# Selecting condition weights in bf16 parts, and a new order for the start of an attention kernel

## The reference, cut to what matters

```python
# x: (32, 32, 512) = batch, channel, time; itok: (32,) in 0..15; all float32
W1 = L0_cond_weights[itok]                   # (32, 32, 32), chosen by the token of each batch
h = einsum('bct,bcd->bdt', x, W1)            # first mix
q, k, v = h @ wq, h @ wk, h @ wv             # 32 query heads, 8 key/value heads of 128
...                                          # rotary embedding, causal softmax, out = att @ v
x = x + out @ wo
W2 = L0_cond2_weights[itok]
y = einsum('bct,bcd->bdt', x, W2)            # second mix
x = x + ffn(y)                               # fp8 rounding of y and of the weight, bias, scale
```

## Time and profile before

| | |
|---|---|
| median of 3 runs | 549.89 us (548.65 to 551.2) |
| the profiled execution | 549.17 us |
| its span | 547.3 us, mean granted clock 0.976 |
| TensorE busy | 521.5 us, 95% of the span |
| VectorE busy | 354.2 us, 65% |
| GpSimd busy | 221.7 us, 40% |
| ScalarE busy | 211.1 us, 39% |
| DMA engines | q1: 26.63 MB, 14.0% of the time of 16 engines |

### The profile page before, as it was taken

One profiled execution on the slowest core, in us unless ns is written; L12 is line 12 of the kernel. 1 busy time (PEld: TensorE's weight loads), 2 busy tenths in 40 slices (PEclk: granted clock), 3 DMA queues, 4 the chain that ended last, 5 costly groups with the idle time before them and its releaser, 6 DMA issues.

```text
span 547.3 us, 8771 instructions
## 1 busy us (share of the span) xinstructions
PE 521.5 (95%) x3208; PEld 416.5 (76%) x3209; DVE 354.2 (65%) x544; ACT 211.1 (39%) x369; POOL 221.7 (40%) x178
## 2 busy tenths in 40 slices
PE   8799999999999999999999999999999999999690
PEld 6687888888888888888888888888888888887320
DVE  5658356666676667666666675667566756675697
ACT  1244224341634163416342535162516251612524
POOL 0035623542663266326722673267326633510002
PEclk9999999999999999999999999999999999999775
DMA  8404400020103010301020102010202000000004
GB/s 265 164 1 153 174 0 2 1 96 2 46 33 96 0 71 6 96 0 77 0 96 0 77 1 94 0 77 18 78 0 77 6 0 1 2 0 1 2 0 153
DMA packets 17662, 26.88 MB, mean 49 GB/s; under 512 B 1611, under 2 KB 5835, under 8 KB 17644
## 3 DMA queue, kind: packets, MB, share of 16 engines
q1 hardware_dynamic: 17644, 26.63, 14.0%
HBM read 24.53 MB, written 2.10 MB: 49 GB/s over the span
## 4 chain that ended last, share of the span: by engine, by line
PE 94%; DVE 4%; DMA 1%; issue 1%; ACT 0%; DVEq 0%; SPq 0%
PE bank L524 25%; PE bank L525 24%; PE bank L526 24%; PE bank L603 3%; PE bank L590 3%; PE bank L544 3%; PE bank L545 3%; PE bank L546 3%; PE bank L718 2%; PE bank L658 1%; PE bank L496 1%; PE bank L507 1%; DVE xacc L999 1%; PE bank L715 1%; DMA cst<-in_constants 1%; DVE v_all L994 1%
## 5 line engine op out<-in xcount | busy, mean ns | idle before, releaser
L814 DVE TENSOR_TENSOR q_cos<-bank,cst 128x512 f32<-128x512 f32 x80 | 55.3, 691 | 105.2 <-ACT q_swap L385 105.2
L293 POOL TENSOR_TENSOR q_rot<-q_cos,q_swap 128x512 f32<-128x512 f32 x64 | 82.5, 1289 | 89.2 <-DVE q_swap L816 89.2
L524 PE MATMUL bank<-wo_hi,o_hi 128*128 128x512 f32 x256 | 101.6, 397 | 1.3 <-issue 1.3
L524 PE MATMUL bank<-hT_hi,wq_hi 128*128 128x512 f32 x256 | 101.3, 396 | 0.0
L525 PE MATMUL bank<-wo_lo,o_hi 128*128 128x512 f32 x256 | 99.8, 390 | 0.0
L525 PE MATMUL bank<-hT_lo,wq_hi 128*128 128x512 f32 x256 | 99.8, 390 | 0.0
L526 PE MATMUL bank<-wo_hi,o_lo 128*128 128x512 f32 x256 | 99.6, 389 | 0.0
L526 PE MATMUL bank<-hT_hi,wq_lo 128*128 128x512 f32 x256 | 99.6, 389 | 0.0
L384 ACT ACTIVATE q_swap<-bank 64x512 f32<-64x512 f32 x80 | 47.6, 595 | 127.3 <-PE bank L526 127.3
L859 DVE TENSOR_TENSOR xacc<-xacc,bank 128x512 f32<-128x512 f32 x64 | 43.4, 677 | 42.7 <-PE bank L526 42.5
L272 POOL TENSOR_TENSOR wo_lo<-raw_o,wo_hi 128x512 fp32r<-128x512 f32 x32 | 43.6, 1387 | 58.7 <-ACT wo_hi L374 58.7
(11 more groups left out here) (126 smaller groups left out, 716.1 us busy)
## 6 DMA issues: line engine op xcount, KB each, us to landing
raw_q<-in_L_attn_wq SPq DMA_DIRECT2D x8, 1024.0 KB, 5.8
raw_o<-in_L_attn_wo SPq DMA_DIRECT2D x8, 1024.0 KB, 5.0
xacc<-in_x SPq DMA_DIRECT2D x4, 512.0 KB, 7.3
raw_k<-in_L_attn_wk SPq DMA_DIRECT2D x8, 256.0 KB, 2.6
out<-xacc SPq DMA_DIRECT2D x8, 256.0 KB, 2.0
raw_o<-in_L_attn_wv SPq DMA_DIRECT2D x1, 1024.0 KB, 8.0
raw_q<-in_L_attn_wv SPq DMA_DIRECT2D x1, 1024.0 KB, 5.9
q_rot<-in_L_ffn_qweight SPq DMA_DIRECT2D x1, 1024.0 KB
```

The lines of the kernel that those rows point to most:

```text
L293: pool.tensor_tensor(dst, q_cos[b][:], q_swap[b][:], ALU.add).then_inc(rope_done, 1)
L524: pe.matmul(dst, l_hi, r_hi, start=(i == 0), stop=False)
L814: dve.tensor_tensor(by_t(q_cos[b][:]), by_t(q_ps[ITEM_BANK[k]][:]), cos_b, ALU.mult).then_inc(rope_cos, 1)
```

## The change

- The condition weights are split into three bf16 parts that add up to them exactly. ScalarE rounds (three casts), VectorE subtracts what has been rounded from `wcond` in place (two *remainder* steps). The parts lie side by side in `wcond_parts`, in `s_exp`.
- The selectors are bf16, which holds 0 and 1 exactly. select(i) is eight bf16 matmuls of 192 columns (3 parts of 64). In spread_first VectorE first adds the three parts with a reduction into `chosen` (in `p_tr`) and then spreads from there; the late spreads read `chosen` too, and no longer PSUM. The fourth select uses bank 3 again and not bank 7.
- ScalarE issues the loads of the small constants and of the condition weights; SP starts with the tokens and goes on with `x`. The first half of the value weights comes in two loads of 512 KB, each behind one of the first two pairs of `x`, with a semaphore of its own.
- The low parts of the first half of the value weights are made by GpSimd, and ScalarE makes the high parts in pairs between the first h_high.
- The orders: TensorE has select 0, mix 0, 1, select 1, mix 2, 3, select 2, values 0, 1, select 3, mix 4, 5, values 2. values(0) no longer waits for the late spreads. VectorE's order is below.

The core of the diff:

```diff
-        sel_ps = [bank[3], bank[4], bank[5], bank[7]]
+        sel_ps = [bank[3], bank[4], bank[5], bank[3]]
...
-            sp.dma_start(cst[:, 0:C_FIRST], consts[:, 0:C_FIRST]).then_inc(dma_cond, 16)
-            sp.dma_start(wcond, cond_v).then_inc(dma_cond_w, 16)
             for t in range(0, TILES, 2):
                 sp.dma_start(xacc[:, t:t + 2, :], x_rows[t:t + 2].rearrange("t p h -> p t h")).then_inc(dma_x[t // 2], 16)
-                if t == 2:
-                    sp.dma_start(raw_o[:], wv_v[:, :, 0:512]).then_inc(dma_wv, 16)
+                if t < 4:
+                    sp.dma_start(raw_o[:, t:t + 2, :], wv_v[:, t:t + 2, 0:512]).then_inc(dma_wv_first[t // 2], 16)
...
+            for c in range(KC):
+                pool.wait_ge(wv_hi_done, c + 1)
+                pool.tensor_tensor(wo_lo[:, c, :], raw_o[:, c, :], wo_hi[:, c, :].bitcast(F32),
+                                   ALU.subtract).then_inc(wv_lo_first, 1)
...
-            for t in range(TPU):
-                h_high(t)
-            for c in range(KC):
-                wv_high(c)
-            for t in range(TPU, TILES):
+            act.dma_start(cst[:, 0:C_FIRST], consts[:, 0:C_FIRST]).then_inc(dma_cond, 16)
+            act.dma_start(wcond, cond_v).then_inc(dma_cond_w, 16)
+
+            for part in range(3):
+                if part == 0:
+                    act.wait_ge(dma_cond_w, 16)
+                else:
+                    act.wait_ge(cond_rest, part)
+                act.activation(wcond_parts[:, :, part, :], wcond, ACT.Copy).then_inc(cond_part, 1)
+            wv_high(0)
+            wv_high(1)
+            h_high(0)
+            h_high(1)
+            wv_high(2)
+            wv_high(3)
+            for t in range(2, TILES):
                 h_high(t)
...
-                        mm = pe.matmul(sel_ps[i][:, half * 64:(half + 1) * 64], selector[i][:, k, half * BPT:(half + 1) * BPT, :],
-                                       wcond[:, k, :], start=(k == 0), stop=(k == 3))
+                        mm = pe.matmul(sel_ps[i][:, half * 192:(half + 1) * 192], selector[i][:, k, half * BPT:(half + 1) * BPT, :],
+                                       wcond_parts[:, k, :, :], start=(k == 0), stop=(k == 3))
...
-                if i == 0:
-                    pe.wait_ge(wbd2_done, TILES // 2)
...
+            def remainder(part):
+
+                dve.wait_ge(cond_part, part)
+                dve.tensor_tensor(wcond, wcond, wcond_parts[:, :, part - 1, :], ALU.subtract).then_inc(cond_rest, 1)
...
             def spread_first(i):
                 dve.wait_ge(sel_mm, i + 1)
+                dve.tensor_reduce(chosen(i), sel_ps[i][:, 0:384].rearrange("p (t s n) -> p t n s", t=2, s=3), AX_X,
+                                  ALU.add).then_inc(sel_sum, 1)
+                dve.wait_ge(sel_sum, i + 1)
                 spread_blocks(i, 0).then_inc(wbd_done, 1)
```

More of the change, by code:

```diff
@@ L142, in build @@
         dma_x = [dma_x] + [sem(f"dma_x{i}") for i in range(1, TILES // 2)]
+        dma_wv_first = [sem(f"dma_wv_first{i}") for i in range(2)]
         dma_qk, dma_o, dma_out = sem("dma_qk"), sem("dma_o"), sem("dma_out")
@@ L178, in build @@
         flat = lambda a: a[:].rearrange("p a t -> p (a t)")
-        selector = [v_all[:, TPU + i, :].rearrange("p (k b c) -> p k b c", k=4, c=T) for i in range(TILES // 2)]
+        selector = [v_all[:, TPU + i, 0:KV * HD // 2].bitcast(BF16).rearrange("p (k b c) -> p k b c", k=4, c=T)
+                    for i in range(TILES // 2)]
         warm = w8[:, 0, :]
@@ L511, in _ @@
             select(0)
-            select(1)
             mix(0)
             mix(1)
-            select(2)
-            select(3)
+            select(1)
             mix(2)
             mix(3)
+            select(2)
             def three_pass(dst, pairs, first_wait=None):
@@ L550, in _ @@
             values(1)
+            select(3)
             mix(4)
@@ L753, in h_low @@
                                   hT_hi[:, :, cols].bitcast(F32), ALU.subtract).then_inc(h_lo_done, 1)
-            def wv_low(c):
-                dve.wait_ge(wv_hi_done, c + 1)
-                dve.tensor_tensor(wo_lo[:, c, :], raw_o[:, c, :], wo_hi[:, c, :].bitcast(F32),
-                                  ALU.subtract).then_inc(wv_lo_first, 1)
             def round_e4m3(dst, scaled, plain, total, done, n):
@@ L775, in v_copy @@
                 dve.tensor_copy(v_all[:, t, n * 512:(n + 1) * 512], v_ps[i % 2][:]).then_inc(v_copied, 1)
+            remainder(1)
             select_pair(dve, 0).then_inc(sel_lhs, 1)
+            remainder(2)
             select_pair(dve, 1).then_inc(sel_lhs, 1)
             spread_first(0)
+            spread_first(1)
             select_pair(dve, 2).then_inc(sel_lhs, 1)
-            spread_first(1)
-            select_pair(dve, 3).then_inc(sel_lhs, 1)
-            spread_first(2)
-            spread_first(3)
             h_low(0)
             h_low(1)
+            spread_first(2)
+            h_low(2)
+            h_low(3)
+            select_pair(dve, 3).then_inc(sel_lhs, 1)
+            spread_first(3)
             for i in range(TILES // 2):
                 spread_blocks(i, 1).then_inc(wbd2_done, 1)
-            h_low(2)
-            h_low(3)
-            for c in range(KC):
-                wv_low(c)
             v_copy(0)
```

15 lines of the change are left out of this document (11 added, 4 removed).

## The result

The changed kernel took **556.06 us** (median of 4 runs, 555.41 to 557.33) against 550.39 us for the kernel before on the same chip (4 runs, 548.65 to 551.2): ratio 1.011, 95% interval 1.0077 to 1.0143. That is slower by more than the 0.5% that a measurement can tell, and above the range of the forecast. The profiled execution took 555.52 us, 1.8 more than its span.

The account below looks back on a forecast made before the run. TensorE, busy for 95% of the span, was taken to bound the kernel, so only its start mattered. A gain of 1.0 to values(0) and a loss of 2.3 to values(2) made +1.3 on 549.89: 551.2 us, range 548.2 to 554.2.

Parts of the forecast that it names:

- rival C: At the start, TensorE's clock falls: +3 to +5 us, 553 to 556, most likely 554.9 us; chance 0.12.
- (a): Landing of the condition weights at the start: 5.9 us, between bounds of 4.8 and 7.0, against 5.26 before.
- (b): Casts, remainders and selector from the landing to select(0): select(0) at 8.9 against 6.64 us, 2.2 late.
- (c): From select(0) to mix(0): reduction, then a spread slowed 1.8 times beside GpSimd to 0.76; mix(0) at 11.2 against 10.26 us.
- (d): From mix(0) to mix(3): slowed second spread, and selector(2) at 2.2 us beside GpSimd's splits; mix(3) at 18.1 us.
- (e): Start of values(0) after mix(3) and select(2): 19.7 against 20.71 us, a gain of 1.0.
- (f): From values(0) to values(2): select(3) and late spreads hold back v_copy(0); 9.6 against 7.23 us, a loss of 2.3.
- The exclusion: The part of the kernel behind 35 us: any difference there was excluded.
- Rival A: At the start, landing near 5 and cheap shared reads: 548.5 to 549.9, most likely 549.2 us; chance 0.25.
- Rival B: At the start, landing at 6.5 to 7.0 and shared-read factor 2.1 to 2.4: 552.4 to 553.6 us; chance 0.22.

Follow-up runs that it names:

- e2: Changed kernel with 28 warm matmuls in place of 11 and 6 more before each of mix(0), mix(2) and mix(3): 552.38 us, ratio 1.0029.
- e9: Changed kernel with the first value splits back on VectorE, two behind the first spread and two behind h_low(1): 554.63 us, ratio 1.0066.
- e6: Changed kernel with the loads of the small constants and condition weights issued by SP ahead of x, not by ScalarE: 554.94 us, ratio 1.007.
- e5: Kernel before with the bf16 selection alone; loads, orders and value splits as before: 549.5 us, ratio 0.9989.
- e11: Kernel before with the bf16 selection, the first value splits moved to GpSimd and the late spreads moved: 547.84 us, ratio 0.9941.
- e12: e11 with 17 warm matmuls in place of 11: 548.0 us, ratio 0.9948.
- e4: Changed kernel with GpSimd's splits held behind the first spread and all four ScalarE high parts ahead of h_high(0): 551.54 us, ratio 1.0012.
- e8: Kernel before, f32 selection kept, first value splits moved to GpSimd and three late spreads behind the value copies: 546.54 us, ratio 0.9931.
- e3: Changed kernel with the four late spreads behind v_copy(0) and v_copy(1) on VectorE: 554.98 us, ratio 1.0069.

## Why the prediction was wrong

**The step that failed: the clock.** The forecast took every TensorE duration of the start at the full clock, and left the fall to rival C, with 0.12. It came, and cost 3.7 us (e2). The forecast of the difference was +1.3; it is +5.7 in the medians, 4.4 more, and +6.4 in the spans of the profiled runs. Along its own marks, in the trace: mix(0) to select(1) 3.57 and not 1.84 (+1.7), the two waits for a select 1.48 and 1.53 and not 0.87 (+1.3), mix(3) 1.84 and not 0.92, select(2) 1.12 and not 0.65 (+1.4): 4.4 us of clock in all. (Values(2) came 5.4 later than forecast; landing and the two spreads make 0.9 of it. That the difference of the medians is off by 4.4 as well is in part chance, since the trace is off by 5.4.) e2 gets less back, since its select(0) comes 0.5 later behind the warm matmuls and its spreads take 0.7 longer.

Why it had only 0.12: rival C was tied to a landing of 6.5 or later, and argued away with the earlier trace rows, where 2.59 us idle left the clock full. Both were wrong readings. The forecast's own gap of 3.0 us (5.88 to 8.9) was the dangerous one already: with gaps of 3.00 (e9) and 2.73 (e6) ahead of select(0) the clock fell too, while with 1.14 (e5), 1.83 (e11) and 1.08 (e12) it did not fall there. And the 2.59 us of the earlier trace rows had heavy selects and mixes ahead of them; with light ones the same wait did bring the clock down (e5, 3.26 us of work for 3.90). The change takes away TensorE work that, by e5, was holding the clock, and this I counted as pure gain. The Trainium skill (TensorE: Matmul & The Clock Gate, What's actually happening) puts it the right way round: the throttled state is the default, and activity releases it. The trace agrees: 1.16 us of work between 18.21 and 21.62, at 1.00, were followed by a clock of 0.50.

**Rival C** was the case that came. Its price, +3 to +5, holds 4.4; its time, 554.9, is 1.2 below the median, and 0.5 of that is the kernel before, whose median is 550.39 now and was 549.89. In the trace values(2) is 6.72 late where rival C has 5.0: the clock took 0.7 more than I had for it, the landing 0.4, the two spreads 0.5.

**(a) Landing** 6.3 for 5.9, inside 4.8 to 7.0. The rule of the Trainium skill that engines take turns between queue rows (DMA: Bandwidth & Descriptors, Queues, rings and completion order) would have given 7.0 by the forecast's estimate; the load came between the two, nearer the forecast. (In that 7.0 the 0.4 us for the report come from no row.) That the load is slower when ScalarE issues it level with x than when SP issues it ahead of x is shown (5.1 to 5.7 against 2.6 to 3.7); whether the queue or the place does it isn't, nor is the turn-taking.

**(b) Parts.** Right: a cast 0.42, a remainder 0.43, the second cast behind the selector, 3.0 us from landing to select(0), 9.35 for 8.9. The gap ahead of it grew to 3.83 since the warm matmuls also ended earlier, at 5.52 for 5.88.

**(c), (d) Shared reads.** Right in kind, and near in sum (4.30 us for 3.7): spreads 1.15 and 0.87 for 0.76, selector 2.28 for 2.2, reduction 0.56 as forecast. But the form was wrong. I took a factor of 1.8, with 2.4 as its end; the first spread took 2.7 times its length and the selector 1.9. What the traces show is a wait to the end of the running split: sixteen spreads that started beside one, over nine kernels, ended 0.27 to 0.29 us behind the end of that split, and seven selectors 1.08 or 1.09 behind it. The loss was 0.26 to 1.07 us for an instruction of 0.42 and 1.06 to 1.07 for one of 1.22, so it went by what was left of the split and not by the instruction's own length. What I didn't see either is that each of these is a gap on TensorE besides, and so feeds the clock: e4 took 2.2 us off VectorE and won 4.5. The Trainium skill (GPSIMD Engine Reference, Key points) names two SBUF inputs as the condition, and here the runs show it for the spread itself: 0.42 from PSUM beside GpSimd in e8, 0.68 to 1.49 from SBUF.

**(e) values(0)** at 25.10 for 19.7: it is the sum of the above.

**(f) What is handed back.** Right: 9.56 us for 9.6, a stop of 1.33 for about 1.7, released by v_copy; e3 gives 1.36 of the 2.33 back. Here select(3) ran at the full clock and took 0.83, the 0.67 and tail of the estimate.

**The exclusion** of a difference behind 35 us held between these two runs, 519.0 against 519.4 us. As a rule it is too strong: the profiled runs of e2 and e5 had 522.0 there, with more work under the low clock of the last 40 us.

**Rival A** failed at each step; e5, with the selection alone, lies in its range, but can't be told from no change. **Rival B** had the contention near its size, a landing 0.2 too late and no fall of the clock, and so a range that ends 2.5 us below the median.

**Still open.** What exactly decides when the clock falls: the runs give the gaps and the work between them, but no run varied one alone. What sets how much work falls under the low clock behind 510 us. Why the medians of e11 and e12 are level. And each clock reading is of one profiled run of its kernel; the other runs show only that the mean clock of the changed kernel was 0.959 to 0.972 in all four.

## What to carry to other kernels

Ahead of a dense stretch, count TensorE's idle time together with how light the work between the gaps is: a change that makes work cheaper and starts it later can cost the clock, and filling only the first gap merely moves the fall. Before work goes to GpSimd, look at what VectorE does in those microseconds: instructions with an operand in PSUM kept their length here, those with both in SBUF waited for the running GpSimd instruction to end, up to 1.07 us each however short they were. And test the parts of a bundle alone: the splits on GpSimd, with the late spreads moved behind the copies, gave 0.7% in the old order; in the new one the same splits cost the two spreads and the selector 2.2 us.

## What the hardware showed beyond the forecast

- The price of a light start is paid later, in dense work too: values(0) of e5 ran without a gap, and still had a granted clock of 0.50 from 19.75 to 23.16, which made it and values(1) 1.65 us longer in sum.
- Two issuing engines: 128 KB in rows of 256 bytes took 5.1 to 5.7 us when ScalarE issued it at 1.19, level with SP's first 512 KB load, and 2.6 to 3.7 when SP issued it at 1.66 ahead of them.
- A load whose landing varies with nothing changed (2.6 to 3.7 us for the same issue) moves the whole start with it: select(0) of e5 and e11, whose issue and casts are the same, stood at 7.42 and 8.18.
- VectorE waits for GpSimd, and GpSimd hardly for VectorE: a spread of 0.42 us took up to 1.49, its end always 0.27 to 0.29 behind that of the split, while four splits took 4.96 us alone or beside PSUM reads and 5.12 to 5.33 beside SBUF reads (the one in whose first part a spread was still at work 1.45 and not 1.26).
- The same part of a program can differ by 3 us between kernels in which nothing of it was changed: 519.0 to 522.0 us behind values(2), with 7 to 15 us of TensorE work under a clock of 0.50 in it.
